# The D part of a state-space mixer summed in PSUM by products with diagonals, and the gate taken over by VectorE

## Reference

```python
z = zxbcdt[..., :D_INNER]                          # the gate, D_INNER = 256
xs = jax.nn.silu(zxbcdt[..., D_INNER:2 * D_INNER]) # 4 heads of 64
...
Yd = jnp.einsum('bhcls,bcshp->bclhp', M, Xc)       # inside a chunk
Yo = jnp.einsum('bcln,bchpn,bhcl->bclhp', Ck, states_in, jnp.exp(A_cs))
y = (Yd + Yo).reshape(B, Ls, NHEADS, HEADDIM) + xh * D[None, None, :, None]
y = y.reshape(B, Ls, D_INNER)
y = y * jax.nn.silu(z)
y = y * jax.lax.rsqrt(jnp.mean(y * y, -1, keepdims=True) + 1e-06) * rms_w
```

## Time and profile before

| | |
|---|---|
| time, median of 3 runs | 411.37 us (410.9 to 412.04) |
| span of the profiled execution | 414.5 us |
| its own time outside the span | none is given |
| busy in the span | PE 349.5, PEld 238.0, DVE 292.3, ACT 235.2, POOL 230.4 us |
| granted TensorE clock | 0.980 mean; full in every slice but the last two of 40 |
| DMA | 41.97 MB, mean 101 GB/s |
| chain that ended last | PE 56%, DVE 20%, issue 7%, POOL 7%, ACT 4% |

### The profile page before, as it was taken

One profiled execution on the slowest core, in us unless ns is written; L12 is line 12 of the kernel. 1 busy time (PEld: TensorE's weight loads), 2 busy tenths in 40 slices (PEclk: granted clock), 3 DMA queues, 4 the chain that ended last, 5 costly groups with the idle time before them and its releaser, 6 DMA issues.

```text
span 414.5 us, 9020 instructions
## 1 busy us (share of the span) xinstructions
PE 349.5 (84%) x2869; PEld 238.0 (57%) x2869; DVE 292.3 (71%) x836; ACT 235.2 (57%) x460; POOL 230.4 (56%) x341
## 2 busy tenths in 40 slices
PE   1999977888988999988878899988997999999900
PEld 1666645556544545444444445567776899898800
DVE  3555645888788888878796736376776877877737
ACT  2677644432667666455577687744644665666514
POOL 2660598855354435271569788546575445445525
PEclk9999999999999999999999999999999999999975
DMA  8933322636515040322624343211112211111054
GB/s 269 336 110 106 87 85 77 187 94 186 171 33 166 5 140 5 99 70 75 196 69 131 117 155 102 74 32 40 53 41 78 78 53 40 53 52 35 32 171 146
DMA packets 44461, 41.97 MB, mean 101 GB/s; under 512 B 4560, under 2 KB 38416, under 8 KB 44416
## 3 DMA queue, kind: packets, MB, share of 16 engines
q1 hardware_dynamic: 41136, 35.10, 28.1%
q0 software_dynamic: 2272, 4.69, 3.2%
q10 hardware_dynamic: 1008, 1.61, 1.1%
HBM read 26.36 MB, written 14.75 MB: 99 GB/s over the span
## 4 chain that ended last, share of the span: by engine, by line
PE 56%; DVE 20%; issue 7%; POOL 7%; ACT 4%; another core or an unknown queue 3%; DMA 2%; ACTq 0%; DVEq 0%; POOLq 0%
PE banks L1017 12%; DVE nm L1210 8%; PE banks L1044 6%; PE banks L1032 4%; PE banks L859 4%; PE banks L698 4%; PE banks L907 3%; PE banks L1045 2%; PE banks L755 2%; PE banks L937 2%; PE banks L763 2%; DVE ctx_in L1152 2%; PE banks L806 2%; PE banks L934 1%
## 5 line engine op out<-in xcount | busy, mean ns | idle before, releaser
L1210 DVE TENSOR_REDUCE nm<-banks 128x4 f32<-128x1024 f32 x64 | 78.1, 1220 | 17.5 <-PE banks L850 11.4
L1520 ACT ACTIVATE probs_all<-banks 128x1024 f32<-128x1024 f32 x64 | 65.4, 1023 | 36.0 <-PE banks L859 29.6
L1017 PE MATMUL banks<-w_split,scores_in 128*128 x234 | 64.5, 410 | 0.0
L1342 DVE TENSOR_TENSOR ctx_in<-ctx_in,banks 128x512 f32<-128x512 f32 x39 | 26.8, 687 | 27.3 <-ACT ctx_in L1567 21.4
L1017 PEld LDWEIGHTS banks<-w_split,scores_in 128*128 128x128 f32 x234 | 40.8, 189 | 7.7 <-issue 0.9
L1705 POOL DMA_INDIRECT slots_dram<-rows,place_u x32 | 31.9, 996 | 23.5 <-DVE count L1302 16.1
L1727 POOL DMA_INDIRECT y_dram<-x,scatter_u x39 | 38.5, 987 | 11.4 <-POOL x L1723 9.7
L1567 ACT ACTIVATE ctx_in<-banks 128x512 f32<-128x512 f32 x39 | 23.3, 599 | 36.7 <-PE banks L1017 31.9
L859 PE MATMUL banks<-scores_in 32*128 32x256 f32 x256 | 32.2, 326 | 12.0 <-ACT probs_all L1520 6.0
L1044 PE MATMUL banks<-w_split,scores_in 128*128 x156 | 39.1, 327 | 2.8 <-ACT scores_in L1573 2.1
L907 PE MATMUL banks<-probs_all,vals 128*9 128x256 f32 x512 | 39.7, 381 | 0.2
(11 more groups left out here) (230 smaller groups left out, 802.2 us busy)
## 6 DMA issues: line engine op xcount, KB each, us to landing
scores_in<-k_dram SPq DMA_DIRECT2D x32, 128.0 KB, 2.7
scores_in<-q_dram SPq DMA_DIRECT2D x32, 128.0 KB, 2.7
ctx_in<-in_L_ffn_w SPq DMA_DIRECT2D x16, 256.0 KB, 2.7
cs_wide<-cs_dram SPq DMA_DIRECT2D x14, 256.0 KB, 3.7
scores_in<-slots_dram SPq DMA_DIRECT2D x39, 65.0 KB, 1.9
k_dram<-split_qk SPq DMA_DIRECT2D x8, 256.0 KB, 2.5
q_dram<-split_qk SPq DMA_DIRECT2D x8, 256.0 KB, 2.3
ctx_in<-in_L_ffn_wo SPq DMA_DIRECT2D x8, 256.0 KB, 2.9
```

The lines of the kernel that those rows point to most:

```text
L1017: m = TE.matmul(up_bank(i, j), xT[:, i % XT, xh, :], all_weights[:, c + j * FF:][:, bass.ds(expert_at[i], FF)], start=n == 0, stop=n == 2)
L1210: V.tensor_reduce(most, maxima_of(n).rearrange("p (j k q) -> p j k q", j=2, k=TPS), AX_X, ALU.max, negate=True).then_inc(s["nmax"], 1)
L1520: C.activation(probs(n).rearrange("p j k q -> p (j k q)"), EXPS, ACT.Exp, scale=SCALE).then_inc(s["probs"], 1)
```

## The change

D goes onto the diagonals of four 128 by 128 matrices, `d_diag`, made once by POOL from the identity. In PE's `mix` eight products of these with xs go into `Y_SUMS` first (`start` on the first head alone), and the eight products with xdt add to them. DVE then multiplies bank by gate straight into `y` and counts `y_gated`; for k = 1 it first adds the bank to `yoff`. POOL makes no `skip` and no longer multiplies by the gate. The semaphore `skip` is gone, and `y_sum` counts the k = 1 tiles alone. PE's wait before tile t is for `y_gated` of the tile before (k = 1), or for the last `y_sum` (k = 0).

```diff
@@ -310,7 +310,7 @@
         yield from half_tile
 
 
-HALF_SET, ZO_SET, E_SET, ZEROS_SET, VALS_ONES, ROUTE_CONSTS, W_OUT_SET = 1, 3, 4, 5, 6, 10, 12
+HALF_SET, ZO_SET, E_SET, ZEROS_SET, VALS_ONES, ROUTE_CONSTS, W_OUT_SET, SKIP_SET = 1, 3, 4, 5, 6, 10, 12, 16
 ONE_SET, SP_IN, DT_READY, A_READY, AV_ZERO = 1, 2, 3, 4, 5
 SP_EXP, SP_LN, NEG_A_EXP, CS_SET, DEC_SET = 1, 2, 3, 4, 7
 SUMS_MM, CS_T = 1, 2
@@ -321,7 +321,7 @@
 SIGNALS = (
     "consts_g steps_pe steps_v steps_a own_v "
     "var own_g rstd xn xn_t hT proj_mm proj dts rot ctx_t cT kv_mm split_hi split_lo valsb "
-    "bc_t bcT score_mm score diff fall xdt skip xdec decay mat state_mm state off_mm "
+    "bc_t bcT score_mm score diff fall xdt xdec decay mat state_mm state off_mm "
     "y_mm y_sum y_gated sq yT_t yT rms_in rms out_mm r1 ln1_var ln1_in ln1 x1 x1_t x1T "
     "q_mm max_mm nmax nm_split nm_t nm_out exp_mm probs av_mm av_lo av_hi heads_t o_norm o_t oT wo_mm "
     "r2 ln2_var ln2_in ln2 x2 x2_t x2T rows_x2 gate_mm logit ge topped chosen rank_mm counted w_hi w_lo "
@@ -436,7 +436,7 @@
         scores = msb("scores", [P, NT, P])
         xdt = msb("xdt", [P, 4, NH, HP])
         xdec = msb("xdec", [P, 2, NH, HP])
-        skip = msb("skip", [P, 4, NH, HP])
+        d_diag = msb("d_diag", [P, NH, P])
         state = msb("state", [P, DI])
         y = msb("y", [P, 2, TPS, DI])
         ysq = msb("ysq", [P, DI])
@@ -792,19 +792,27 @@
             def mix(t):
                 b, k = divmod(t, TPS)
                 r, ring = t % 3, t % 4
-                q.wait_ge(s["y_sum"], t)
+                if k == 1:
+                    q.wait_ge(s["y_gated"], t)
+                else:
+                    q.wait_ge(s["y_sum"], b)
                 q.wait_ge(s["steps_a"], DEC_SET)
+                q.wait_ge(s["consts_g"], SKIP_SET)
                 if k == 1:
                     at, g = in_group(t)
                     q.wait_ge(s["state"], b + 1)
                     TE.matmul(Y_SUMS[:, DI:2 * DI], bcT[at, g, 1, :], state[at, :], start=True, stop=True,
                               tile_position=(at.start, 0)).then_inc(s["off_mm"], 1)
+                for h in range(NH):
+                    for rows in COLUMN_HALVES:
+                        TE.matmul(Y_SUMS[rows, h * HP:(h + 1) * HP], d_diag[:, h, rows], proj[:, t, DI + h * HP:DI + (h + 1) * HP],
+                                  start=h == 0, stop=False, tile_position=(0, rows.start), skip_group_check=True)
                 q.wait_ge(s["mat"], t + 1)
                 q.wait_ge(s["xdt"], t + 1)
                 for h in range(NH):
                     for rows in COLUMN_HALVES:
                         m = TE.matmul(Y_SUMS[rows, h * HP:(h + 1) * HP], decay[:, r, h, rows], xdt[:, ring, h, :],
-                                      start=True, stop=True, tile_position=(0, rows.start))
+                                      start=False, stop=h == NH - 1, tile_position=(0, rows.start), skip_group_check=True)
                 m.then_inc(s["y_mm"], 1)
 
             def turn_mixed(b):
@@ -868,7 +876,7 @@
                     slots = 2 if later - LEAD > LAST_MIXER else 1
                     q.wait_ge(s["nmax"], later - slots + 1)
                     if second_slot(later):
-                        q.wait_ge(s["y_sum"], NT)
+                        q.wait_ge(s["y_sum"], B)
                         mix_bank.wait()
                     q.wait_ge(s["score"], GROUP)
                 if n is not None:
@@ -1154,8 +1162,8 @@
 
             def mix(t):
                 b, k = divmod(t, TPS)
-                bb, ring = b % 2, t % 4
-                add = skip[:, ring].rearrange("p h c -> p (h c)")
+                bb = b % 2
+                inner = Y_SUMS[:, 0:DI]
                 q.wait_ge(s["y_mm"], t + 1)
                 if k == 1:
                     q.wait_ge(s["off_mm"], b + 1)
@@ -1164,14 +1172,12 @@
                         yoff[:, :].rearrange("p (h c) -> p h c", h=NH), Y_SUMS[:, DI:2 * DI].rearrange("p (h c) -> p h c", h=NH),
                         ecs[:, t, :].unsqueeze(2).to_broadcast([P, NH, HP]), ALU.mult))
                     own.settle()
-                    q.wait_ge(s["skip"], t + 1)
-                    own.step(V.tensor_tensor(yoff[:, :], yoff[:, :], add, ALU.add))
-                    own.settle()
-                    add = yoff[:, :]
-                q.wait_ge(s["skip"], t + 1)
+                    V.tensor_tensor(yoff[:, :], inner, yoff[:, :], ALU.add).then_inc(s["y_sum"], 1)
+                    q.wait_ge(s["y_sum"], b + 1)
+                    inner = yoff[:, :]
                 q.wait_ge(s["yT_t"], b - 1)
                 q.wait_ge(s["sq"], TPS * (b - 1))
-                V.tensor_tensor(y[:, bb, k, :], Y_SUMS[:, 0:DI], add, ALU.add).then_inc(s["y_sum"], 1)
+                V.tensor_tensor(y[:, bb, k, :], inner, proj[:, t, 0:DI], ALU.mult).then_inc(s["y_gated"], 1)
 
             def mix_residual(b):
                 bb = b % 2
@@ -1637,19 +1643,12 @@
                 q.wait_ge(s["y_mm"], t - 3)
                 q.wait_ge(s["xdec"], (t - 4) // TPS + 1)
                 G.tensor_tensor(xdt[:, r], xs, dts[:, t, :].unsqueeze(2).to_broadcast([P, NH, HP]), ALU.mult).then_inc(s["xdt"], 1)
-                q.wait_ge(s["y_sum"], t - 3)
-                G.tensor_tensor(skip[:, r], xs, d_skip[:, :].unsqueeze(2).to_broadcast([P, NH, HP]), ALU.mult).then_inc(s["skip"], 1)
                 if k == 0:
                     q.wait_ge(s["xdt"], t + 1)
                     q.wait_ge(s["steps_a"], DEC_SET)
                     q.wait_ge(s["state_mm"], b - 1)
                     G.tensor_tensor(xdec[:, b % 2], xdt[:, r],
                                     dec[:, t, :].unsqueeze(2).to_broadcast([P, NH, HP]), ALU.mult).then_inc(s["xdec"], 1)
-
-            def mix(t):
-                b, k = divmod(t, TPS)
-                q.wait_ge(s["y_sum"], t + 1)
-                G.tensor_tensor(y[:, b % 2, k, :], y[:, b % 2, k, :], proj[:, t, 0:DI], ALU.mult).then_inc(s["y_gated"], 1)
 
             def turn_mixed(b):
                 bb = b % 2
@@ -1744,7 +1743,10 @@
             G.tensor_scalar(count[:, :], iota[:, 0:NE], float(EXPERT_ROWS), float(P), ALU.mult, ALU.add).then_inc(s["consts_g"], 1)
             for c in range(2):
                 G.tensor_scalar(w_out[:, c, :], w_out[:, c, :], rms_w[:, c:c + 1], 0.5 * float(np.sqrt(DI)), ALU.mult, ALU.mult).then_inc(s["consts_g"], 1)
-            middle = dict(mask_decays=mask_decays, scale_inputs=scale_inputs, mix=mix, turn_mixed=turn_mixed,
+            q.wait_ge(a["w_first"], W_FIRST)
+            for h in range(NH):
+                G.tensor_scalar(d_diag[:, h, :], ident, d_skip[:, h:h + 1], 1.0, ALU.mult, ALU.mult).then_inc(s["consts_g"], 1)
+            middle = dict(mask_decays=mask_decays, scale_inputs=scale_inputs, turn_mixed=turn_mixed,
                           mix_residual=mix_residual, out_project=out_project, split_maxima=split_maxima, choose=choose, place_chosen=place_chosen,
                           split_weights=split_weights, down=down)
             for stage, *at in middle_order():
```

## The result

The changed kernel takes 413.44 us (median of 4 runs, 412.73 to 414.24), the kernel before 411.55 us beside it (4 runs, 410.9 to 412.04). The ratio is 1.0043, with a 95% interval of 1.0025 to 1.006: 1.9 us slower by the medians, between 1.0 and 2.5 by the interval. The forecast was 415.4, 4.0 us slower. The profiled execution of the changed kernel took 412.73 us, with a span of 411.3 us.

The account below looks back on a forecast made before the run. POOL and PE were taken to bound the first regime (51 to 76.5 us), PE and DVE in turn the second (to 178). First regime -1.7, products +6.0, port relief -0.3 gave +4.0: 415.4 us, range 413.7 to 417.3.

Parts of the forecast that it names:

- Direction and place: Whole mixer part: POOL time saved from 51 to 76.5 us, PE time paid from 76.5 to 178; +4.0 us.
- Rival 1: PE's idle from 76.5 to 178 us takes in the new products; 6.0 us fall away, 409.4 us; chance 0.13.
- rival 4: Before the first row maximum nothing is gained, PE becoming its bound or products costing more; +6.2, 417.6 us; chance 0.06.
- rival 2: From 76.5 to 178 us half of the new products are hidden; +1.0, 412.4 us; chance 0.16.
- The sign that I gave, the new line on the chain in nine tiles: From tile 6 on, PE's new line stands on the chain next to line 806 in nine tiles.
- the price of the group, 0.62 us: PE's eight new products per tile cost 0.62 us; nine groups on the chain, 5.6 us.
- First regime, -1.7: From 51 to 76.5 us, without POOL's gate and skip, the first maximum comes 1.7 us earlier.
- Tile 10, 0.4: Tile 10's group is off the chain, with some 0.2 us to spare on PE; it costs 0.4 us.
- Port relief, 0.3: DVE instructions shorten without POOL's work beside them; one at 151.27 us counts, 0.3 us gained.
- rival 3: DVE's relief from POOL comes in full, 4.7 us, line 1152's median falling to 0.68; 411.0 us; chance 0.07.
- POOL's four products, nothing: POOL's four diagonal matrices, made at 28.2 us, take 1.7 us inside 15.7 us of idle; cost nothing.
- the shift stays: After 178 us nothing of the change is left, so the +4.0 us carries to the end.

Follow-up runs that it names:

- pool_gate: Changed kernel with the gate multiplication given back to POOL and three more unread products on PE; ratio 1.0044 to the kernel before, 412.9 us.
- vector_gate: Kernel before with the gate moved to DVE, skip left on POOL, no diagonal products, three more unread products on PE; ratio 1.0122, 417.4 us.
- after_warm: Changed kernel with three more unread products in PE's stops before the second and fifth row maxima; ratio 1.0032 to the kernel before, 414.9 us.
- after_fewer: Changed kernel with three more unread products early and one fewer at each of six later steps; ratio 0.9969 to the kernel before, 412.0 us.
- first_six_fewer: Change in tiles 0 to 5 alone, kernel before elsewhere, three more unread products early, one fewer at six later steps; ratio 0.9933, 408.9 us.
- after_again: Changed kernel run once more, unaltered, beside the kernel before on another chip; ratio 1.0063, 415.8 us.
- first_six_warm: Change in tiles 0 to 5 alone, kernel before elsewhere, with three more unread products in PE's early stops; ratio 1.0035, 413.7 us.
- before_fewer: Kernel before with three more unread products early and one fewer at each of six later steps; ratio 1.0005, 412.0 us.

## Why the prediction came out as it did

**Direction and place: right.** The time grew, through a trade of POOL's time in the first regime against PE's time in the second, and in the second each of tiles 6 to 15 adds its own step. Rival 1 (PE's idle takes the products in) and rival 4 (no gain in the first regime) did not happen. Nor did rival 2, though the time, 413.44, lies nearer to its 412.4 than to the 415.4 of the forecast: no tile hid its group, each cost less. The sign that I gave, the new line on the chain in nine tiles, came in eight.

**The step that failed: the price of the group, 0.62 us.** I took it from the chain's piece for line 806, and wrote beside it that the array's mode does not change between the two groups, "so no further break" (the pieces are 0.61 to 0.64 us, not up to 0.66). The consequence was not drawn: if 0.62 holds a break that is paid once, the second group costs 0.62 less that break. It is 0.47, by the chain of the changed kernel and by the 32 instructions in 1.08 us with doubled products. That makes 4.7 in place of 6.0. My bounds for the term, 5.6 to 6.2, left out the true value, and the wider bound of zero was used for a rival only. The Trainium skill, "TensorEngine Tiling (Array Packing)", section "Key Properties", says that changing the tiling mode drains the engine. The trace agrees in so far as 0.15 us comes with the change of shape and not with the second group; no run separates a drain from other causes of it. The Trainium skill, "VectorE: DVE Perf Modes", section on the TRN2 errata, gives a matmul max(60, 6 + columns) cycles at 2.4 GHz, an estimate of 29 ns for 64 columns and 0.47 us for sixteen. The trace has 0.47 for this shape, but it doesn't bear the rule out for others: of the fp32 products over the whole array four instructions of 256 columns take 1.06 us, 265 ns each, where an estimate by it is 109. So the agreement may be chance, and the price is better read from the doubled group.

**First regime, -1.7: right in size, half right in cause.** Measured -1.61, with the steps at 58.2, 68.55 and 73.9 where I had 59.2, 69.2 and 74.2. That the end agrees is in part luck: the first step came 1.0 us earlier than worked out (three groups on the way at 0.15 us less each are 0.45 of it), and from there to the last it took 0.7 longer, with the norm's DVE pair, 1.20 us in the kernel before, at 1.63. But I had the gate as the first cause, and pool_gate has all but 0.1 us of the gain with the gate still on POOL (as a balance, see there). In vector_gate the gate's removal alone gave nothing, though there DVE was burdened too, so it isn't a clean test of the gate. So the skip's removal is enough for nearly all of the gain; that the gate's alone would not have been is not shown. With both gone and no new products the gain is 2.46 us, and the products take 0.85 back, where I had put their busy time at 3.1.

**Tile 10, 0.4: right** (0.45). Tile 10 stands on the chain like the others now.

**Port relief, 0.3: too small.** The lines that answer to rows 9 (ns min/median/max):

```profile
L1160 DVE TENSOR_TENSOR ctx_in<-ctx_in,scores x16: 673/682/1096, 48.9 to 164.5; 128x512 f32<-128x512 f32 x16
L1201 DVE TENSOR_SCALAR x<-r,mv,rs x16: 333/452/1077, 61.9 to 188.5; 128x128 f32<-128x128 f32 x16
```

The median of line 1152 went from 0.872 to 0.682 us, which is the sign that I had given for rival 3. Its price did not come: two of these instructions were on the way of a maximum, at 99 us (1.00 us on the chain, now 0.60) and at 151 us (1.54, now 0.68), and gave 0.7 us together, 0.33 and 0.37; behind the others no lasting step of the maxima is seen. Line 1195 got no shorter (0.420, now 0.452). The prediction had only the one at 151 us, for 0.3. A median moves with many instructions, and the time with those on the chain: the sign was badly chosen.

**POOL's four products, nothing: right.** They take 1.41 us from 28.19 us on, and POOL then still waits 14.2 us for its next work.

**After 178 us, "the shift stays": shown among later versions, not against the kernel before,** of which both profiles have the stops. Three profiles have the clock at 1.00 up to 390 us and different shifts: from after_warm to after_fewer 2.23 us at the 40th maximum are 2.45 at the end, from after_fewer to first_six_fewer 3.14 are 3.03. After_warm and the first result, equal at the 40th, are 0.8 us apart at the end, so that much is between executions. The sum up to the 40th, +2.40, is within the measured 1.0 to 2.5, so nothing large comes after it on the whole. But execution by execution the granted clock moves the time there by as much as the change. That was in none of my cases: each was worked out at full clock, since the profile of before showed 1.00 in both regimes. The forecast's own range, 413.7 to 417.3, missed the time by 0.3 us; that the wider one, 410.8 to 417.4, held it is owed to rivals 2 and 3, not to a case that knew the cost.

## What to carry to other kernels

When a group of like instructions on TensorE is doubled, price the second group by the rate inside a group, not by the chain's piece, which here held 0.15 us at its start that is paid once; look in the trace for a line with more of them back to back, or double the group in a run. Work moved from a waiting engine to TensorE pays only in the stretch where TensorE waits for that engine: here a version that moves it in six tiles of sixteen beats both kernels (0.9933 of the time before) with the unread products that fill TensorE's stops re-dealt, which alone gave nothing (1.0005). Before a gain of under 1% is believed, see how the granted clock spreads over the executions: here a fall of it costs as much as the change.

## What the runs showed of the hardware

- **The granted clock falls after stops of TensorE of about 0.7 to 2.4 us, but not each time.** A stop of 1.18 us that ended at 84 us was followed by 1.00 in one execution and by 0.50 (1.2 GHz) in another of the same program. A stop of 2.14 us that ended at 314 us in the first profile of the kernel before was followed by 1.00, one of 0.69 us at 125 us in after_again by 0.50. In vector_gate it fell behind stops of 1.98 and 1.88 us; the falls between 214 and 228 us came behind stops of 0.96 us (first_six_warm) and of 1.05 and 1.11 us, then 0.73 (pool_gate, before_fewer). Up to 390 us the clock stayed down for 3.4 us at the shortest and 10.3 at the longest. With the stop filled to 0.31 us it stayed at 1.00 in that place. The Trainium skill, "TensorE: Matmul & The Clock Gate", section "What's actually happening", says that what watches the engine runs free of the kernel and does not start with it; that one program gives both outcomes agrees.
- **DVE and ACT can stop together, with no cause in the trace.** The first profile of the kernel before, and all four on the slower chip, have stops of 1.4 to 3.0 us of both engines, ended by what the profile calls "remote", at the same three maxima and at a few places behind them, as at 180.73 us above (1.91 on DVE; ACT's stop before 180.61 is 2.41 us). The other nine profiles have none. The kernel before with other unread products has none on another chip, and three versions of the changed one have them on the slower chip: they are of the chip or the execution, not of the kernel. What they are stays open.
- **A DVE instruction with two inputs in SBUF** took 0.42 us alone (84.13 us) and 0.83 beside POOL's `skip` and `xdec` (66.10 us), both line 1177 in vector_gate.
